# The first layer's gate and scan output turned to run by features, its output projection in three parts

## The reference

```
xz = rmsnorm(x) @ in_proj_w.T + in_proj_b     # 512 -> 3072
x, z = xz[..., :1536], xz[..., 1536:]
u = silu(causal conv of 4 taps over x + conv_b)
xp = u @ x_proj_w.T + x_proj_b                # per head: dt, B (64), C (64)
B, C = B / max(norm(B), 1e-12), C / max(norm(C), 1e-12)
per head (24 heads, 64 wide) and position t:
    alpha_t = clip(base + (1 - base) * relu(tanh(beta * surprise(dt, B, mean(u)))), .01, .999)
    h = alpha_t * h + (1 - alpha_t) * outer(B_t, u_t)
    y_t = C_t @ h
out = (Y * silu(z)) @ out_proj_w.T + out_proj_b
result = x + res_gate * out
```

## Time and profile before

| | us |
|---|---|
| three runs, median (lowest to highest) | 5138.81 (5133.1 to 5145.39) |
| the profiled execution, whole | 5107.47 |
| its span on the core | 5105.8 |
| busy in it: PE, DVE, ACT, POOL | 4036.0 (79%), 2823.3 (55%), 1618.9 (32%), 1412.4 (28%) |
| the three functions of the change | 0 to about 1968 |

### The profile page before, as it was taken

How to read it: one execution, slowest core, us unless ns; L and a number is a source line. 1 busy time by engine, 2 the same in 40 slices (tenths; PEclk the granted TensorE clock), 3 DMA queues, 4 the chain that set the end, 5 groups by cost and what they waited for, 6 DMA issues and landing times. The chain is left out here.

```text
span 5105.8 us, 61033 instructions
## 1 busy us (share of the span) xinstructions
PE 4036.0 (79%) x19166; PEld 3090.8 (61%) x19166; DVE 2823.3 (55%) x5022; ACT 1618.9 (32%) x3311; POOL 1412.4 (28%) x1213
## 2 busy tenths in 40 slices
PE   7985999979999796852995886677778778837993
PEld 6874777767777544642442775455556556715772
DVE  6664344443444344972223674899999855532335
ACT  4342222232222110020221565555555422203431
POOL 0001200000000003755102440899999800011002
PEclk9997999989999898965997898898889989968996
DMA  4224622232122343133996534332222021133324
GB/s 129 104 100 175 198 81 79 65 103 83 58 86 74 109 187 129 45 142 103 339 318 223 167 121 150 117 138 93 82 79 78 28 99 52 49 97 112 116 95 120
DMA packets 434226, 603.28 MB, mean 118 GB/s; under 512 B 115142, under 2 KB 310791, under 8 KB 424849
## 3 DMA queue, kind: packets, MB, share of 16 engines
q1 hardware_dynamic: 388240, 490.99, 29.3%
q0 software_dynamic: 43232, 101.96, 6.0%
q10 hardware_dynamic: 2592, 8.39, 0.4%
HBM read 436.56 MB, written 206.54 MB: 126 GB/s over the span
## 5 line engine op out<-in xcount | busy, mean ns | idle before, releaser
L2216 PE MATMUL d_py<-d_h,d_ident 128*128 128x256 f32 x2048 | 543.5, 425 | 176.4 <-POOL d_h L2056 156.7
L2064 POOL TENSOR_TENSOR d_dBu<-d_B,d_dtu 128x1024 f32<-128x1024 f32 x256 | 596.8, 2362 | 115.4 <-DMA d_dtu<-dtu 115.4
L2216 PEld LDWEIGHTS d_py<-d_h,d_ident 128*128 128x128 f32 x2048 | 431.1, 214 | 288.3 <-POOL d_h L2056 184.6
L715 PE MATMUL a_pB<-a_uhi,a_whi 128*128 128x512 f32 x1152 | 487.7, 423 | 40.9 <-DVE a_ulo L598 40.8
L715 PE MATMUL a_pB<-a_uhi,a_wlo 128*128 128x512 f32 x1152 | 461.6, 401 | 0.0
L715 PE MATMUL a_pB<-a_ulo,a_whi 128*128 128x512 f32 x1152 | 458.7, 398 | 0.0
L2102 ACT ACTIVATE d_ph<-d_dt,d_A 128x255 f32<-128x255 f32 x1024 | 425.7, 460 | 0.1
L2162 DVE TENSOR_TENSOR_SCAN d_ph<-d_ph,d_dBu 128x1024 f32<-128x1024 f32 x160 | 365.7, 2286 | 18.4 <-POOL d_dBu L2064 12.0
L1004 POOL TENSOR_TENSOR b_kv<-b_c 128x128 f32 (+11 forms) x256 | 100.3, 431 | 864.6 <-DMA b_c<-ctx_turned 860.7
L715 PEld LDWEIGHTS a_pB<-a_uhi,a_whi 128*128 128x128 f32 x1152 | 223.4, 194 | 83.3 <-issue 31.7
L682 DVE SCALAR_TENSOR_TENSOR a_W<-a_pG,a_cB,a_M 128x256 f32<-128x256 f32 (+1 forms) x384 | 142.7, 413 | 229.7 <-PE a_pG L736 129.9
(11 more groups left out here) (459 smaller groups left out, 9409.5 us busy)
## 6 DMA issues: line engine op xcount, KB each, us to landing
c_gu<-w_gu SPq DMA_DIRECT2D x64, 768.0 KB, 5.1
a_wraw<-w_bc SPq DMA_DIRECT2D x24, 1536.0 KB, 5.9
a_alall<-alpha SPq DMA_DIRECT2D x24, 1024.0 KB, 5.9
slots<-a_zeros POOLq DMA_DIRECT2D x64, 256.0 KB, 3.4
c_wd<-w_down SPq DMA_DIRECT2D x64, 256.0 KB, 6.1
c_xb<-slots SPq DMA_DIRECT2D x64, 256.0 KB, 8.0
slots_y<-c_y POOLq DMA_DIRECT2D x64, 256.0 KB, 7.1
f_w1r<-w SPq DMA_DIRECT2D x64, 256.0 KB, 2.6
```

The costliest lines, as they stand in the source:

```text
L715: ins = nc.tensor.matmul(out, a[:, k, cols], b[:, k, ts], start=(k == 0 and n == 0), stop=(k == F - 1 and n == 2))
L2064: pool.tensor_tensor(dBu[c % RB][:, :, :], B_sb[i][:, q * G:(q + 1) * G, :], dtu_sb[i][:, f, :].unsqueeze(1).to_broadcast([P, G, L]), ALU. ...
L2216: ins = nc.tensor.matmul(py[f % 2][:, 0:L], ident_sb[:, :], h_sb[c % RH][:, n, :], start=False, stop=(q == Q - 1 and n == G - 1))
```

## The change

**In `ssm0_project`** z is made by features: for every f, right after px, PE makes pz with W stationary and 256 columns of x passing; ACT applies silu with the bias straight from PSUM, in its order ahead of u of the same g = f-1, and DVE's addition is gone. PE's pz(f) waits for the silu of f-2. z is stored by features.

**In `ssm0_scan`** the output is made by features: u is stationary (64 columns, one head), W passes with 128 columns, and the two heads write the two halves of py's partitions; six matmuls for each sequence, from four buffers of W. 1/|C| then lies along the columns: SP stores it to DRAM and loads it back spread over 64 partitions for each head, at the start of each of its steps. DVE multiplies once per sequence, at odd i. y is stored by features. u comes in chunks of 256 KB through six buffers; the weights of B and of C are loaded apart into one buffer half as wide; the constants come behind the first weights; the zeros come from one half of a constant tile, 128 columns repeated.

**In `ssm0_out`** the transposes and their copies are gone. y and z are multiplied in two pieces of six groups, ACT rounds to y_hi, DVE makes y_lo, and PE makes po from 72 parts. The weights are loaded in 12 chunks through four buffers and split the same way during batch 0; the residual x is loaded apart from y and z.

```diff
-                sp.wait_ge(s_z, b * 6 + 6)
-                sp.dma_start(z_tok[bass.ds(b * L, L), :].rearrange("(c p) n -> p c n", p=P), z_sb[:, :, :]).then_inc(s_out_z, 16)
+                sp.wait_ge(s_z, b * F + F)
+                alone(sp, tick_sp)
+                sp.dma_start(z_feat[:, :, bass.ds(b * L, L)].rearrange("k p t -> p k t"), z_sb[:, :, :]).then_inc(s_out_z, 16)
...
                     if f >= 1:
                         g = f - 1
+                        if g == 0:
+                            act.wait_ge(s_out_z, b * 16)
+                        act.wait_ge(s_pz, b * F + g + 1)
+                        nc.scalar.activation(z_sb[:, g, :], pz[g % 2][:, 0:L], ACT.Silu, bias=bz_sb[:, g:g + 1]).then_inc(s_z, 1)
...
-                    if f % 2:
-                        n = f // 2
-                        pe.wait_ge(s_zb, b * 6 + max(n - 1, 0))
-                        c, j = n // 3, n % 3
-                        if first and n < 3:
-                            ready(pe, 3 + j)
-                        for k in range(KD):
-                            ins = parts(pz[n % 2][:, :], (xnT_hi, xnT_lo), slice(c * P, (c + 1) * P), (w_hi, w_lo), slice(DI + j * BANK, DI + (j + 1) * BANK), k)
-                        ins.then_inc(s_pz, 1)
+                    pe.wait_ge(s_z, b * F + max(f - 1, 0))
+                    if first and f % 4 == 0:
+                        ready(pe, 3 + f // 4)
+                    for k in range(KD):
+                        ins = parts(pz[f % 2][:, 0:L], (w_hi, w_lo), slice(DI + f * P, DI + (f + 1) * P), (xnT_hi, xnT_lo), slice(0, L), k)
+                    ins.then_inc(s_pz, 1)
...
+            def b_weights(pair, parity):
+                sp.dma_start(w_raw[:, :, :], w_bc[bass.ds(pair, 1), :, :, B_COLS].rearrange("a p k n -> (a p) k n")).then_inc(s_w, 16)
                 sp.dma_start(bias_sb[parity][:, :], b_bc[bass.ds(pair, 1), :, :].rearrange("a p n -> (a p) n")).then_inc(s_w, 16)
+
+            def c_weights(pair, unit):
+                sp.wait_ge(s_wl, unit * 2 + 1)
+                alone(sp, tick_sp)
+                sp.dma_start(w_raw[:, :, :], w_bc[bass.ds(pair, 1), :, :, C_COLS].rearrange("a p k n -> (a p) k n")).then_inc(s_w, 16)
+
+            def consts():
+                sp.dma_start(idz[:, 0:P], ident).then_inc(s_const, 16)
+                sp.dma_start(pair_sb[:, :], head_pair).then_inc(s_const, 16)
+                sp.dma_start(dtm_sb[:, :, :], dt_mean.rearrange("c p h -> p c h")).then_inc(s_const, 16)
+                for n, v in enumerate((b_dt, a_log, l2_alpha, l2_beta, ema)):
...
+            def norms(cur):
+                sp.wait_ge(s_rC, cur + 1)
+                alone(sp, tick_sp)
+                sp.dma_start(norm_rows.rearrange("r t -> t r"), rC[:, :, :].rearrange("p h c -> p (h c)"), allow_slow_non_contiguous=True).then_inc(s_rC_stored, 16)
+                sp.wait_ge(s_rC_stored, cur * 16 + 16)
+                alone(sp, tick_sp)
+                for h in range(2):
+                    sp.dma_start(rC_all[h * S:(h + 1) * S, :], norm_rows[h * TT:(h + 1) * TT, :].rearrange("c t -> (c t)").partition_broadcast(S)).then_inc(s_rC_all, 16)
+
             def step(half, cur, nxt, parity=None, first=False):
                 into, at = parities(nxt, cur, parity)
                 pair = None if nxt is None else nxt - half * PAIRS
+                if cur is not None:
+                    norms(cur)
...
+                        b_weights(0, into)
+                        c_weights(0, 0)
+                        consts()
...
-                            pool.dma_start(rows[bass.ds(r * ZERO_ROWS * P, ZERO_ROWS * P), :].rearrange("(p c) n -> p c n", p=P), zeros[:, :, :]).then_inc(s_clear, 16)
+                            pool.dma_start(rows[bass.ds(r * P, P), :].rearrange("p (c n) -> p c n", n=P), zeros).then_inc(s_clear, 16)
...
-                    if j >= 2:
-                        pool.wait_ge(s_ul, j - 1)
-                    pool.dma_start(u_raw[j % 2][:, :, :], u_feat[k:k + KC, :, half * TH + n * BANK:half * TH + (n + 1) * BANK]
-                                   .rearrange("k p t -> p k t")).then_inc(s_u[j % 2], 16)
+                    if j >= UBUF:
+                        pool.wait_ge(s_ul, j - UBUF + 1)
+                    pool.dma_start(u_raw[j % UBUF][:, :, :], u_feat[k:k + KC, :, half * TH + n * BANK:half * TH + (n + 1) * BANK]
+                                   .rearrange("k p t -> p k t")).then_inc(s_u[j % UBUF], 16)
...
-                    if i >= 2 and i % 2 == 0:
-                        b = i // 2 - 1
+                    if i >= 3 and i % 2 == 1 or i == NI:
+                        b = (i - 3) // 2 if i < NI else NBH - 1
                         if b == 0:
                             dve.wait_ge(s_out, cur * 16)
-                        dve.wait_ge(s_y, cur * NI + i)
-                        pyb = py[:, 0:L].rearrange("p (h c n) -> p h c n", h=2, c=2)
-                        for h in range(2):
-                            ins = nc.vector.tensor_tensor(y_sb[:, 2 * b:2 * b + 2, h * S:(h + 1) * S], pyb[:, h, :, :],
-                                                          rC[:, h, 2 * b:2 * b + 2].unsqueeze(2).to_broadcast([P, 2, S]), ALU.mult)
-                        ins.then_inc(s_ye, 1)
+                            dve.wait_ge(s_rC_all, cur * 32 + 32)
+                        dve.wait_ge(s_y, cur * NBH + b + 1)
+                        nc.vector.tensor_tensor(y_sb[:, b * L:(b + 1) * L], py[:, 0:L], rC_all[:, b * L:(b + 1) * L], ALU.mult).then_inc(s_ye, 1)
...
-                def output(i):
-                    b, h = i // 2, i % 2
-                    pe.wait_ge(s_W, cur * NI + i + 1)
-                    if h == 0:
-                        pe.wait_ge(s_ye, cur * NBH + b)
-                    o = h * 2 * S
-                    u0, u1 = ut_sb[at][:, 2 * b, h * S:(h + 1) * S], ut_sb[at][:, 2 * b + 1, h * S:(h + 1) * S]
-                    nc.tensor.matmul(py[:, o:o + S], W[i % 2][:, 0:P], u0, start=True, stop=True)
-                    nc.tensor.matmul(py[:, o + S:o + 2 * S], W[i % 2][:, P:2 * P], u0, start=True, stop=False)
-                    nc.tensor.matmul(py[:, o + S:o + 2 * S], W[i % 2][:, 2 * P:3 * P], u1, start=False, stop=True).then_inc(s_y, 1)
+                def output(b):
+                    pe.wait_ge(s_W, cur * NI + 2 * b + 2)
+                    pe.wait_ge(s_ye, cur * NBH + b)
+                    for lo, w0, w1, c, start, stop in ((0, 0, P, 0, True, True), (P, P, 2 * P, 0, True, False), (P, 2 * P, 3 * P, 1, False, True)):
+                        for h in range(2):
+                            r = slice(h * S, (h + 1) * S)
+                            ins = nc.tensor.matmul(py[r, lo:lo + P], ut_sb[at][:, 2 * b + c, r], W[(2 * b + h) % 4][:, w0:w1], start=start, stop=stop)
+                    ins.then_inc(s_y, 1)
...
+            load(0, 0)
+            for k in range(F):
+                if k >= WBUF:
+                    sp.wait_ge(s_wl, k - WBUF + 1)
+                sp.dma_start(w_raw[k % WBUF][:, :], w_out[k * P:(k + 1) * P, :]).then_inc(s_w[k % WBUF], 16)
+            load(1, 1)
             for i in range(2):
-                load(i, i)
-            with sp.Fori(0, NB // 2 - 1) as r:
-                for i in range(2):
-                    b = 2 * r + i
+                residual(i, i)
+            sp.wait_ge(s_yl, 2)
+            load(2, 0)
+            for b in range(NB):
+                if b + 3 < NB:
+                    sp.wait_ge(s_yl, b * 2 + 4)
+                    alone(sp, tick_sp)
+                    load(b + 3, (b + 1) % 2)
...
+                for n, ks in enumerate(PIECES):
+                    act.wait_ge(s_yz, b * 2 + n + 1)
                     if n == 0:
-                        act.wait_ge(s_o, b * 2)
-                    nc.scalar.copy(yT[:, n // 3, (n % 3) * 4:(n % 3) * 4 + 4, :].rearrange("p k t -> p (k t)"), pT[n % 2][:, :]).then_inc(s_yT, 1)
-
+                        act.wait_ge(s_o, max(b * 2 - 2, 0) if isinstance(b, int) else b * 2 - 2)
+                    nc.scalar.copy(y_hi[i][:, ks, :], y_sb[i][:, ks, :]).then_inc(s_yh, 1)
...
+                for ks in PIECES:
+                    nc.vector.tensor_tensor(y_sb[i][:, ks, :], y_sb[i][:, ks, :], z_sb[i][:, ks, :], ALU.mult).then_inc(s_yz, 1)
+                for n, ks in enumerate(PIECES):
+                    dve.wait_ge(s_yh, b * 2 + n + 1)
+                    nc.vector.tensor_tensor(y_lo[i][:, ks, :], y_sb[i][:, ks, :], y_hi[i][:, ks, :].bitcast(F32), ALU.subtract).then_inc(s_yl, 1)
...
-                for n in range(6):
-                    c, j = n // 3, n % 3
-                    pe.wait_ge(s_yz, b * 2 + c + 1)
-                    pe.wait_ge(s_yT, b * 6 + max(n - 1, 0))
-                    for q in range(4):
-                        ins = nc.tensor.transpose(pT[n % 2][:, q * P:(q + 1) * P], y_sb[i][:, c, (j * 4 + q) * P:(j * 4 + q + 1) * P], ident_sb[:, :])
-                    ins.then_inc(s_T, 1)
```

(33 more changed lines are left out.)

162 lines of the change are left out of this document (79 added, 83 removed).

## The result

The changed kernel took 5158.31 us in the median of 9 runs (5153.37 to 5166.6), the kernel before 5144.99 in the median of 9 (5133.1 to 5154.19): a ratio of 1.003, with a 95% interval of 1.0019 to 1.004. It is slower by about 0.3%, where 1% faster was forecast.

The account below looks back on a forecast made before the run. PE was taken to set the scan's pace, idling in five places. Terms 7 − 24 − 45 − 6 + 9.5 + 10.5 = −48 took the median 5138.8 to 5091 us; forecast's own range 5065 to 5120, 8-in-10 range 5052 to 5155.

Parts of the forecast that it names:

- term 4: Turn of the halves: 36 us instead of 42 through more buffers and one multiplication fewer, −6; clearing stores hidden or 5 us.
- the second rival: Scan units: the round trip of 1/|C| becomes every unit's wait; +66 at 27 us, so 5157; chance 9%.
- term 3: Output in 22 overlapped units: column halves run in pairs and PE's wait for W goes, −2.06 a unit, −45.
- Term 2: Start of the scan: with six buffers loads run ahead and ACT's rounding sets the pace, −24, bounds −5 and −28.
- Term 6: Output projection: PE idles 9.2 us a batch behind a longer loop, 28.2 us a batch instead of 25.2, +10.5.
- Terms 1 and 5: First function: PE waits 2.2 us instead of 1.2 for z's silu, +7; last unit: y waits for 1/|C|, +9.5.
- The column halves one after another: Scan output: the paired matmuls on two column halves run serially, +11 instead of −45, so 5147; chance 15%.
- the loads that do not overlap: Scan output: each of twelve passes pays its own 0.111 us load, +174, so 5265; chance 3%.
- The projection does stall: Rival denying a stall in the output projection: ACT's and DVE's steps beside PE's products, 19.2 us a batch, 5037; chance 9%.

Follow-up runs that it names:

- e13: Changed kernel with only its 80 clearing stores moved to the middles of five batches of the first function, in 2 KB pieces: 5134.42 us, 0.9968 of the kernel before.
- e2: Kernel before with its clearing stores' zeros taken from 128 columns repeated, in pieces of 512 bytes: 5148.21 us, 1.0002 of the kernel before.
- e4: Changed kernel with PE's last square sums of a unit behind nine parts of the next projection: 5109.48 us, 0.9929 of the kernel before.
- e6: Kernel before with PE's last square sums of a unit behind nine parts of the next projection: 5095.51 us, 0.9894 of the kernel before.
- e14: Changed kernel with PE's last square sums of a unit behind three parts of the next projection: 5122.54 us, 0.9943 of the kernel before.
- e3: Changed kernel with ACT's rounding of y(b+2) ahead of its copy of turned result b in the output projection: 5103.33 us, 0.9922 of the kernel before.
- e11: Changed kernel with square sums behind nine parts, ACT's rounding before its copy, second batch's loads earlier, clearing stores in mid-batch of the first function: 4994.1 us, 0.9717.
- e5: Changed kernel with the 80 clearing stores spread over the scan's first half, eight behind each unit's output: 5150.7 us, 1.0004 of the kernel before.
- e9: Changed kernel with the clearing stores in the first function, sixteen at the ends of five batches: 5183.43 us, 1.0068 of the kernel before.

## Why the prediction was wrong, by its steps

- **The failed step is the sentence on the 80 clearing stores in term 4**, "hidden in the first units of the second half or costs up to 5 us", kept outside the sum. The place was wrong as well, there and in the words on the kernel before: the stores stand between the halves in the program, but POOL waits ahead of them only for the zeros and issues them at 486 to 582 us, beside the first overlapped unit of the first half, as it did before. The unit grew by 33 us in the profile; with the stores moved the kernel is 30 us faster in the medians (e13). One half of the mechanism is the second rival's, the round trip of 1/|C| as DVE's wait: I put it in every unit at 9%, and it came in one unit, for 15.0 us of PE. The other half, 19.3 us of PE, stood in no term: term 3 has B's weights behind the round trip in SP's queue, "near 900 and used near 909", 9 us to spare, which holds with free queues only. No run puts B's weights ahead of the round trip, so this division rests on the trace. The loss needed two parts of the change that I had weighed apart: the stores alone cost nothing (e2), the round trip alone, with the queues free, nothing either (e13). With it gone the change is faster by 0.3%, still not by the 1% of the forecast: the unit is half of the 72 us between forecast and profile, and the terms below are the rest.
- **Term 3, −45: the 20 plain units came to −23.5, where it had −41.** The column halves run at once, and the wait for W is gone. A clean unit gained 2.0, where I had 2.06. What failed is that I counted with clean units on both sides. The trace of before already had units of 50.1 us in it; I took 48.6 from one pair of stores. The pause of 1.4 us at the end of a unit brought the lower clock in 8 of 20 units before and 17 of 20 after: 0.8 us a unit given back. e4, e6 and e14 show that it hangs on that pause; that the share of units went from 8 to 17 is explained by no run.
- **Term 2, −24, came to −13.9**: for the reason given for its small end. Transfers pace the chunks, and C's weights were rounded at 461.91 instead of near 453.5; 3 of these 8 us are the first function's.
- **Term 6, +10.5, came to +17.4**: the loop was right in kind (8.8 us idle, 9.2 forecast), and e3 takes it away. Of the missing 7 us 4.8 are in the loop, six batches of 29.0 instead of 28.2, since every second one spends more at the lower clock. The other 2.4 are in the first two batches, which ended 5.0 us earlier than before and not 7.4; ahead of the second DVE waited for z, loaded behind twelve chunks of weights.
- **Terms 1 and 5** had their mechanism: PE's wait ahead of pz(7) was 2.04 us where I had 2.2, the last unit cost 9.5. That the last hit its figure is luck: 1/|C| was ready 1.8 us later behind the store of alpha, its round trip was 0.8 shorter and the rest of the unit 1.0. The first function gained 1 us in its first batch and lost 0.6 in each of the others: +3.1.
- **Term 4, −6**, came to almost nothing (83.5 to 85.2 us for the turn, then 47.0 to 43.7); no run here took it apart.
- **The rivals.** The column halves one after another, and the loads that do not overlap: the twelve instructions in 0.88 us rule out both. The Trainium skill ("TensorE: Matmul & The Clock Gate", part 3, "The mechanism") lets a load overlap only when the row group differs; here all six use all rows and the trace does not agree: the six pairs alone take 0.64 of the 0.80 us, which leaves no room for loads of 0.145 us in the mean that overlap with nothing. That a change of the tiling mode drains the engine stands in the Trainium skill ("TensorEngine Tiling (Array Packing)") under "Key Properties", and not where the prediction has it; no run here isolates its price. The projection does stall in the changed kernel, so that rival fell, but e3 shows that the stall was one of order.

## What to carry to other kernels

A store and reload through DRAM in pieces of a few bytes can take three times as long amid bulk stores (32.5 us here instead of 10.3), and what stands behind it in the same queue, here B's weights, comes late with it. Before adding one, look for the bulk transfers that have no deadline and ask when each is issued, then move those to a place where nobody waits for a landing (e11: for nothing; e5 and e9: the same stores for 25 and 50 us). Count units over many periods, not one, and look for a slow clock behind each pause of the bounding engine: moving 1.4 us of waiting was worth 2.3 us a unit in the kernel before and 3.5 in the changed one (e6, e4). Where three engines pass work around, put what depends on the next batch ahead of what waits for the last one.

## What was not expected of the hardware

- Two matmuls of 128 passing columns on the two column halves of the array run together, weight loads included: 0.80 us for twelve instructions (the output of one sequence at 847.97).
- The landing of a store of 4-byte pieces went from 10.3 us with free queues (1703.07 to 1713.40, last unit) to 32.5 with them full, while alpha's store of the same kind took only 12.7 in the kernel before amid the same stores. The row holds the 24 stores and the 48 quick loads behind them:

```profile
DMA to landing us min/median/max: 3.4/4.3/32.5
```

- The lower clock came 3 us long behind a pause of 1.36 us in 17 of 20 units of the changed kernel and in 8 of 20 of the kernel before. Behind one of 0.67 us, three parts later in the order, it came in none of the ten plain units of the second half (e14).
